# Key and query loads gated one by one on the next batch's scores, weights in six portions

## The chip, the core and the metric

One NeuronCore of a Trainium2 chip runs the whole program. The metric is the device time in microseconds (us) of one execution, lower is better. PE is the matmul engine (PEld its weight loads), DVE, ACT and POOL are the vector, scalar and GpSimd engines, SP is the sync engine, which here only waits and issues DMAs.

## The reference

Two transformer layers over x of 16 batches x 112 tokens x 256, with a context of 16 x 375 x 256. Layer 0 has a linear cross-attention and a mixture of 8 experts; layer 1 has a softmax cross-attention (the "second attention") and a feed-forward with low-rank experts. The part that matters:

```python
x = x + _L1_xattn_ref(_layernorm(x), ctx_1024, Wq, bq, Wk, bk, Wv, bv, Wo, bo)
#   Q, K, V = split into 16 heads of 16;  scores = Q K^T / 4
#   weights = softmax(scores);  attn = weights V;  return attn @ Wo.T + bo
x = x + _L1_ffn_ref(_layernorm(x), wi, bi, wo, bo, lora_A, lora_B, gate_w, gate_b)
#   gates from a top-2 of 8;  inter = h wi^T + bi + (h A_e^T) B_e^T
#   out += gate_e * (relu(inter) wo^T + bo)
```

## The kernel before

The stages run one after another: first attention, routing (in which the second attention's keys are made), the experts, the second attention (its queries first, then a loop over the 16 batches from 437 to about 655 us), and the last feed-forward.

**Operands of the second attention.** Keys and queries are split into three bf16 parts each and stacked on the partitions, so that one bf16 matmul gives an exact-enough product. The parts lie in DRAM (`kparts_d`, `qparts_d`). For each batch `load_keys` brings them into `kpk` with three DMAs (for r = 3, 2, 1: 562.5, 375 and 187.5 KB) and `load_queries` into `qpk` with three more (168, 112, 56 KB), 1.46 MB in all. Both tiles have `AHEAD` = 3 slots; batch b lies in slot b % 3.

**A step of the loop.** PE's `step(n)` makes the 12 units of `transposed_scores(n, u)` (four 128x125 by 128x112 matmuls each, line L2035), and after units 2, 4, 6, 8, 10 a pair of plain scores of the next batch (`score(n + 1, j)`, L2010), from which DVE takes row maxima (L1855). ACT takes exponentials of the units (L1756, into `probs`). Each unit adds one to the semaphore `st_ps`. Then come `weigh(n, 0)` (L2048), `shift_turn(n + 1)` (L2019), the first two score pairs of batch n + 2, `weigh(n, 1)`, and `add_up` (L2061). The first pair of scores of a batch is where PE waits for its loads:

```python
if j == 0:
    pe.wait_ge(kpk_in[s].sem, kpk_in[s].at(n // AHEAD))
    pe.wait_ge(qpk_in[s].sem, qpk_in[s].at(n // AHEAD))
```

All instructions of PE stand in this order in its queue, as they do on the other engines.

**The sync queue.** It holds the loads, the stores of query parts (`store(b)`) and the weight loads, each in order. For each n it waits until all 12 units of batch n are done, which frees the slot, and issues the six loads of batch n + 3 (L725, L1599). The stores of batches 10 to 15 stand behind the loads of n = 0 to 2. Once, at n = 9, the six weights of the last feed-forward leave (L1640): lora_a, wg1, wi (1024 KB), lora_b (512 KB), wo (1024 KB), c_earlier, 2.7 MB together. They are laid over `ctx_all`, whose values of batches 0 to 7 must have been copied by then (`vz_done`). ACT waits for the weights (`w_in`) in step 13.

Of the kernel before, what the change touches and what calls it, by code (L numbers as in the profile page):

```python
# [26 lines left out]
B, SQ, SK, D, H = 16, 112, 375, 256, 16  # L27
HD = D // H
T = B * SQ
KC = D // 128  # L30
KT, NKT = 125, 3
E0, F0 = 8, 1024
CAP = T // E0
FC = F0 // 128
E1, R1 = 8, 16
# [8 lines left out]
NR = 3  # L44
# [5 lines left out]
AHEAD = 3  # L50
VW = NKT * D
# [7 lines left out]
SCORES_AFTER, OUT_AT = {2: 2, 4: 3, 6: 4, 8: 5, 10: 6}, 6  # L59
INVERT_AT, NORM_AT = 2, 3  # L60
STATS_AHEAD = 5
WEIGHTS_AT, SPLIT_FROM, TEAM_STATS, TEAM_NORMAL = 9, B - 3, B - 3, B - 2
SPREAD = (slice(0, 4), slice(4, 8), slice(8, 16))


# [10 lines left out]
class Chain:  # L76
# [11 lines left out]
    def next(self):  # L88

        self.marked += 1  # L90
        return self.sem
# [14 lines left out]
def two_layer_kernel(nc, d, out):  # L106
# [5 lines left out]
    kparts_d = dram("kparts_d", [B, KC, NR, HD, H // KC, SK], BF16)  # L112
    qparts_d = dram("qparts_d", [B, KC, NR, HD, H // KC, SQ], BF16)

    def sb(ctx, name, shape, dt=F32, side="left"):
        return ctx.enter_context(nc.sbuf_tensor(name, shape, dt, side=side))
# [525 lines left out]
    rows = sb(ctx, "rows", [SQ, 2, 2, D])  # L642
# [25 lines left out]
    kpk = sb(keys_ctx, "kpk", [128, AHEAD, H, SK], BF16, side="right")  # L668
# [3 lines left out]
    kpk_in = [sem(ctx, f"kpk_in{s}", 48) for s in range(AHEAD)]  # L672
# [43 lines left out]
        act.wait_ge(v_ps.sem, v_ps.at(b))  # L716
        act.activation(ctx_all[0:KT, b], flat[0:KT, at:at + VW], ACT.Copy).then_inc(v_done.sem, 1)

    def load_keys(sp, b):

        s = b % AHEAD
        rows_of = lambda ap, r: ap.rearrange("m r d h k -> (r d) m (h k)")[0:r * HD]
        at = 0
        for r in (3, 2, 1):
            sp.dma_start(kpk[at:at + r * HD, s].rearrange("p (m h) k -> p m (h k)", m=KC),  # L725
                         rows_of(kparts_d[b], r)).then_inc(kpk_in[s].sem, 16)
            at += r * HD

    stage = ExitStack()
    block = stage.enter_context(nc.Block())  # L730
# [240 lines left out]
    @block.sync  # L971
    def _(sp):
        for b in range(AHEAD):
            load_keys(sp, b)
        with sp.Fori(0, E0 // 2 - 1) as i:
            for s in range(2):
                sp.wait_ge(fc2_ps.sem, fc2_ps.at(2 * i + s))
                sp.dma_start(we[:, s], d["we"][2 * i + 2 + s]).then_inc(we_in[s].sem, 16)
# [212 lines left out]
    used = [0]  # L1191

    def over_values(shape):

        size = int(np.prod(shape[1:]))
        view = ctx_all[:].rearrange("p b w -> p (b w)")[0:shape[0], used[0]:used[0] + size]
        used[0] += size
        assert used[0] <= B * VW
        names = "abcd"[:len(shape) - 1]
        spec = "p (" + " ".join(names) + ") -> p " + " ".join(names)  # L1200
        return view.rearrange(spec, **dict(zip(names, shape[1:])))

    wi = over_values([128, KC, F0])
    wo = over_values([128, FC, D])
    la = over_values([128, KC, E1 * R1])
    lb = over_values([E1 * R1, F0])
    wg1 = over_values([128, KC, E1])
    earlier = over_values([SQ, E1, E1])
    covered = (used[0] - 1) // VW
    TEAMS = [range(0, 2), range(2, 6), range(6, 10), range(10, 14), range(14, 16)]  # L1210
    NT, MOST = len(TEAMS), 4
    hn = over_values([SQ, MOST, D])
# [21 lines left out]
    low1_0 = sb(root, "low1_0", [E1 * R1, 2, 2 * SQ], F32R)  # L1234
    low21_0 = sb(root, "low21_0", [E1 * R1, 2, 2 * SQ], F32R)
    bo_f, bg1 = rows1[:, D:2 * D], rows1[:, 2 * D:]
    weights = [(la, "lora_a"), (wg1, "wg1"), (wi, "wi"), (lb, "lora_b"), (wo, "wo"), (earlier, "c_earlier")]
    tile_sum = sb(ctx, "tile_sum", [KT, KC, HC * SQ])
    half_sum = sb(ctx, "half_sum", [KT, KC, HC * SQ])
    probs = sb(ctx, "probs", [KT, KC, NKT, HC * SQ])  # L1240
# [10 lines left out]
    w_in = sem(root, "w_in", 16)  # L1251
# [23 lines left out]
    vz_done = sem(ctx, "vz_done")  # L1275
    st_ps = sem(ctx, "st_ps", UNITS)
# [313 lines left out]
    @block.sync  # L1590
    def _(sp):
        def load_queries(b):

            s = b % AHEAD
            rows_of = lambda ap, r: ap.rearrange("m r d h q -> (r d) m (h q)")[(NR - r) * HD:]
            sp.wait_ge(q_out[b % 2].sem, q_out[b % 2].at(b // 2))
            at = 0
            for r in (3, 2, 1):
                sp.dma_start(qpk[at:at + r * HD, s].rearrange("p (m h) q -> p m (h q)", m=KC),  # L1599
                             rows_of(qparts_d[b], r)).then_inc(qpk_in[s].sem, 16)  # L1600
                at += r * HD

        def store(b):
            i, s = divmod(b, 2)
            sp.wait_ge(qp1_done.sem, qp1_done.at(i))
            sp.wait_ge(qp2_done.sem, qp2_done.at(i))
            sp.wait_ge(qp3_done.sem, qp3_done.at(i))
            if i:
                sp.wait_ge(q_out[s].sem, q_out[s].at(i - 1))
            sp.dma_start(qparts_d[b].rearrange("m r d h q -> (d h) (m r) q"),  # L1610
                         qp[:, i, :, :, s * SQ:(s + 1) * SQ].rearrange("p m r q -> p (m r) q"))\
                .then_inc(q_out[s].sem, 16)

        sp.wait_ge(added.sem, added.at(E0 - 1))
        for g, part in enumerate(GROUPS):
            sp.dma_start(x_all[:, part], by_token(sum_d)[:, part]).then_inc(x2_in[g].sem, 16)
        sp.dma_start(halves[:], d["c_halves"]).then_inc(tables2_in.sem, 16)
        sp.wait_ge(ones_done.sem, ones_done.at(0))
        for s in range(1, AHEAD):
            sp.dma_start(kpk[ROWS:, s], kpk[ROWS:, 0]).then_inc(tables2_in.sem, 16)  # L1620
        for b in range(2):
            store(b)
        for b in range(2):
            load_queries(b)
        for b in range(2, 4):
            store(b)
        load_queries(2)
        for b in range(4, 10):
            store(b)
        for n in range(B):  # L1630
            if n + AHEAD < B:
                sp.wait_ge(st_ps.sem, st_ps.at(n))
                load_keys(sp, n + AHEAD)
                load_queries(n + AHEAD)
            for b in range(10 + 2 * n, min(12 + 2 * n, B)):
                store(b)
            if n == WEIGHTS_AT:
                sp.wait_ge(vz_done.sem, vz_done.at(covered))
                for dst, name in weights:
                    sp.dma_start(dst[:], d[name]).then_inc(w_in.sem, 16)  # L1640

    def unit(u):

        m, rest = divmod(u, NKT * (HC // HU))
        return (m, *divmod(rest, HC // HU))
# [48 lines left out]
    def _(act):  # L1694
# [23 lines left out]
        def zero_padded(n):  # L1718

            act.wait_ge(v_done.sem, v_done.at(n))  # L1720
            if n >= 2:
                act.wait_ge(pv_ps.sem, pv_ps.at(n - 2))
            src = ctx_all[0:KT, n].rearrange("p (t g h e) -> p t g h e", t=NKT, h=2, e=HD)
            for h in range(2):
                ins = act.activation(vz[:, n % 2, :, :, h, h * HD:(h + 1) * HD], src[:, :, :, h], ACT.Copy)
            ins.then_inc(vz_done.sem, 1)
# [13 lines left out]
        def add_bias(n):  # L1740

            act.wait_ge(au_done.sem, au_done.at(n))
            if n:
                act.wait_ge(wo1_ps.sem, wo1_ps.at(n - 1))
            for m in range(KC):
                ins = act.activation(aT1[:, m], au[:, m], ACT.Identity, bias=bv1[:, m:m + 1])
            ins.then_inc(aT1_done.sem, 1)

        def step(n):
            for u in range(UNITS):  # L1750
                m, t, g = unit(u)
                act.wait_ge(st_ps.sem, st_ps.at(n, u + 1))
                if t == 0 and g == 0 and n:
                    act.wait_ge(pv_ps.sem, pv_ps.at(n - 1, m + 1))
                    act.wait_ge(tile_sum_done.sem, tile_sum_done.at(n - 1, 2 * (m + 1)))
                act.activation(probs[:, m, t, g * HU * SQ:(g + 1) * HU * SQ],  # L1756
                               banks[B_ST[u % 3]][0:KT, 0:HU * SQ], ACT.Exp, scale=SCALE)\
                    .then_inc(exp1_done.sem, 1)
                if u == 5 and n:
                    add_bias(n - 1)  # L1760
                if u == 8 and n + 1 < B:
                    zero_padded(n + 1)
                if u == 2 and n >= SPLIT_FROM:
                    if n == SPLIT_FROM:
                        act.wait_ge(w_in.sem, w_in.at(len(weights), 0))
                        for p in range(2):
                            act.wait_ge(q_out[p].sem, q_out[p].at(PAIRS - 1))
                    for k in SPLITS_OF[n]:
                        split_high(act, k)
                if n + 1 == B:  # L1770
                    if u == 1:
                        team_turned(act, 0)
                    if u == 4:
                        low_high(act, 0)
                    if u == 6:
                        gate_exp(act, 0)
            if n + 1 < B:
                spread_shift(n + 1)
# [5 lines left out]
        for n in range(B):  # L1784
            step(n)
# [680 lines left out]
```

## Time and profile before

| | us |
|---|---|
| median of 3 runs | 805.25 |
| lowest, highest | 801.63, 809.89 |
| the profiled execution: time | 802.6 |
| its span in the trace | 800.7 |

The span is that of the instructions; the time has about 2 us more around it. Times in the rows are us from the span's start. In a timeline, neighbouring instructions of one kind are merged into one row (x2 is two of them); the brackets hold the idle time of the engine before it and what ended that. "issue" means that nothing that the profile shows was missing.

### The profile page before, as it was taken

What the parts mean: (1) busy time and instruction counts of PE and PEld (TensorE: products, weight loads), DVE (VectorE), ACT (ScalarE), POOL (GpSimd) and SP (SyncE); (2) the same over time, 40 slices, a digit from 0 to 9 for tenths busy, and PEclk for the clock granted to TensorE, in tenths of its full rate; (3) what the DMA queues carried; (4) which work ended last, traced back from release to release, by engine and by line L of the source; (5) the groups of instructions that cost most, each with busy time, mean ns of one, the idle gap of its engine ahead of it and who ended that gap; (6) DMA issues with size and microseconds to landing.
All of it is one profiled execution on the core that took longest, in us unless ns stands there. A gap on an engine that the chain in (4) does not pass through costs nothing. (4 is left out here: it accounts for less than half of the span.)

```text
span 800.7 us, 16596 instructions
## 1 busy us (share of the span) xinstructions
PE 720.1 (90%) x6421; PEld 609.7 (76%) x6421; DVE 511.8 (64%) x1262; ACT 331.8 (41%) x685; POOL 302.0 (38%) x222
## 2 busy tenths in 40 slices
PE   4899999949998999999878999899978887999997
PEld 3678888724587889988666777777766786898997
DVE  4689888768862233313457777777758758577564
ACT  2122222117833112221336787677857742423223
POOL 2233343327841323222532867677656400000000
PEclk9999999969999999999988999999999999999999
DMA  9994000124777445541642787486953000000000
GB/s 299 358 165 48 23 24 24 47 73 145 202 175 139 140 142 167 190 130 12 128 105 49 125 155 143 91 144 113 255 99 59 2 3 8 4 25 0 25 12 24
DMA packets 64474, 81.54 MB, mean 102 GB/s; under 512 B 31890, under 2 KB 54802, under 8 KB 62834
## 3 DMA queue, kind: packets, MB, share of 16 engines
q1 hardware_dynamic: 61170, 72.22, 38.0%
q0 software_dynamic: 2816, 3.67, 2.5%
q10 hardware_dynamic: 416, 4.65, 1.5%
q8 instruction: 50, 0.82, 0.5%
q14 instruction: 22, 0.18, 0.1%
HBM read 60.45 MB, written 19.31 MB: 100 GB/s over the span
## 5 line engine op out<-in xcount | busy, mean ns | idle before, releaser
L1855 DVE TENSOR_REDUCE mx<-psum 112x2 f32<-112x750 f32 x128 | 113.3, 925 | 17.7 <-PE psum L2010 17.0
L1756 ACT ACTIVATE probs<-psum 125x448 f32<-125x448 f32 x192 | 92.8, 542 | 19.2 <-PE psum L2035 17.4
L556 PE MATMUL psum<-w_parts,c_parts 128*125 128x512 f32 x288 | 75.0, 414 | 10.8 <-DVE w_parts L424 10.4
L1675 POOL TENSOR_TENSOR half_sum<-probs 125x896 f32<-125x896 f32 x30 | 62.5, 2083 | 57.4 <-ACT probs L1756 57.4
L2035 PEld LDWEIGHTS psum<-qpk,kpk 128*125 128x125 bf16 x768 | 62.9, 141 | 22.6 <-issue 14.7
L2035 PE MATMUL psum<-qpk,kpk 128*125 128x112 bf16 x768 | 69.4, 227 | 9.0 <-issue 7.0
L556 PEld LDWEIGHTS psum<-w_parts,c_parts 128*125 128x125 f32 x288 | 54.6, 193 | 25.1 <-DVE w_parts L424 10.4
L2010 PE MATMUL psum<-kpk,qpk 96*112 96x375 bf16 x256 | 64.2, 344 | 9.4 <-DVE mx L1855 8.8
L1681 POOL TENSOR_TENSOR tile_sum<-half_sum,probs 125x896 f32<-125x896 f32 x30 | 62.6, 2087 | 2.4
L1148 PE MATMUL psum<-we,hT 128*112 128x256 f32 x256 | 60.9, 400 | 0.0
L995 ACT ACTIVATE hT<-psum,b 128x224 f32<-128x224 f32 x64 | 25.1, 443 | 77.8 <-PE psum L1133 77.8
L1148 PEld LDWEIGHTS psum<-we,hT 128*112 128x112 f32 x256 | 47.8, 189 | 10.9
L1412 ACT ACTIVATE ctx_all<-psum,cols 128x448 f32<-128x448 f32 (+1 forms) x40 | 22.4, 560 | 80.4 <-PE psum L1576 80.3
L1028 POOL DMA_INDIRECT sum_d<-outs,idx_add x16 | 29.8, 1864 | 63.4 <-DVE outs L1084 51.0
L803 PE MATMUL psum<-ctx_all,wk 128*128 128x375 f32 x128 | 45.5, 500 | 6.4 <-PEq L248 4.9
L2324 PE MATMUL psum<-wo_parts,hs_parts 128*112 128x256 f32 x384 | 48.1, 281 | 3.1 <-DVE wo_parts L1367 3.0
L1133 PE MATMUL psum<-rT,we 128*128 128x224 f32 x256 | 49.8, 353 | 0.9 <-ACT rT L986 0.9
L1080 DVE TENSOR_TENSOR tmp<-psum,b 112x512 f32<-112x512 f32 x8 | 5.5, 691 | 69.1 <-PE psum L1148 69.1
L1133 PEld LDWEIGHTS psum<-rT,we 128*128 128x128 f32 x256 | 48.4, 190 | 1.5 <-issue 1.1
L2324 PEld LDWEIGHTS psum<-wo_parts,hs_parts 128*112 128x112 f32 x384 | 46.1, 175 | 3.9 <-DVE wo_parts L1367 3.2
L1524 DVE SCALAR_TENSOR_TENSOR ctx_all<-psum,neg_bi,ctx_all 128x448 f32<-128x448 f32 (+1 forms) x40 | 23.5, 589 | 37.7 <-PE psum L1585 37.3
L708 PE MATMUL psum<-wv,ctx_all 128*125 128x256 f32 x192 | 47.1, 406 | 0.0
(231 smaller groups left out, 1468.9 us busy)
## 6 DMA issues: line engine op xcount, KB each, us to landing
we<-in_we SPq DMA_DIRECT2D x6, 2048.0 KB, 8.6
kparts_d<-kp SPq DMA_DIRECT2D x16, 562.5 KB, 4.8
kpk<-kparts_d SPq DMA_DIRECT2D x16, 562.5 KB, 6.0
ctx_all<-in_ctxT SPq DMA_DIRECT2D x16, 375.0 KB, 5.2
kpk<-kparts_d SPq DMA_DIRECT2D x16, 375.0 KB, 7.7
we<-in_we ACTq DMA_DIRECT2D x2, 2048.0 KB, 11.9
kpk<-kparts_d SPq DMA_DIRECT2D x16, 187.5 KB, 8.5
qparts_d<-qp SPq DMA_DIRECT2D x16, 168.0 KB, 3.0
```

Of the source, the lines that this page charges most:

```text
L556: ins = pe.matmul(banks[B_KV[t]][0:KT, :], parts_of[:, x, k, t * KT:(t + 1) * KT], w_parts[:, k, w], start=(k == 0 and (x, w) == SPLIT[0]) ...
L708: ins = pe.matmul(flat[0:KT, at + t * D:at + (t + 1) * D], ctx_of(b)[:, k, t * KT:(t + 1) * KT], wv1[:, k], start=(k == 0), stop=(k == KC ...
L803: ins = pe.matmul(banks[B_K[2 * s + m]][:, 0:SK], wk1[:, k, m * 128:(m + 1) * 128], ctx_of(n)[:, k], start=(k == 0), stop=(k == KC - 1))
L1133: ins = pe.matmul(banks[B_F[g]][:, (f % 2) * CAP:(f % 2 + 1) * CAP], we1[:, s, k, f * 128:(f + 1) * 128], rT[:, s, k], start=(k == 0), sto ...
L1148: ins = pe.matmul(banks[B_OUT[s]][0:SQ, h * D:(h + 1) * D], hT[:, s, f, h * SQ:(h + 1) * SQ], we2[:, s, f], start=(f == 0), stop=(f == FC ...
L1675: pool.tensor_tensor(half_sum[:, m], probs[:, m, 0], probs[:, m, 1], ALU.add)\
L1681: pool.tensor_tensor(tile_sum[:, m], half_sum[:, m], probs[:, m, 2], ALU.add)\
L1756: act.activation(probs[:, m, t, g * HU * SQ:(g + 1) * HU * SQ], banks[B_ST[u % 3]][0:KT, 0:HU * SQ], ACT.Exp, scale=SCALE)\
L1855: dve.tensor_reduce(mx[:, n % 2, H + 2 * j:H + 2 * j + 2], psum[0:SQ, first:first + 2, 0:SK], AX.X, ALU.max)\
L2010: ins = pe.matmul(banks[B_S[j % 2] + h][0:SQ, 0:SK], qpk[0:ROWS, s, 2 * j + h], kpk[0:ROWS, s, 2 * j + h], start=True, stop=True)
L2035: ins = pe.matmul(banks[B_ST[u % 3]][0:KT, c * SQ:(c + 1) * SQ], kpk[:, s, h, t * KT:(t + 1) * KT], qpk[:, s, h], start=True, stop=True)
L2324: ins = pe.matmul(y_of(i, s), hs_parts[:, x, f, s * SQ:(s + 1) * SQ], wo_parts[:, w, f], start=(f == 0 and (x, w) == SPLIT[0]), stop=(f == ...
```

## The change

`load_keys` is cut into its three DMAs. In the loop over n each of them waits for a unit of the *next* batch: the first for one finished unit of batch n + 1, the second for three, the third for four; the three query loads follow after five. Before, all six waited for the last unit of batch n. The weights no longer leave together at n = 9 but behind the loads of n = 3 to 8: wi in two halves (512 KB each), wo in two halves, lora_a with wg1 (136 KB), lora_b with c_earlier (540 KB). Each portion waits for the values that it covers. ACT's wait in step 13 counts eight DMAs instead of six.

```diff
+KEYS_AT, QUERIES_AT = (1, 3, 4), 5
-    def load_keys(sp, b):
-
-        s = b % AHEAD
-        rows_of = lambda ap, r: ap.rearrange("m r d h k -> (r d) m (h k)")[0:r * HD]
-        at = 0
-        for r in (3, 2, 1):
-            sp.dma_start(kpk[at:at + r * HD, s].rearrange("p (m h) k -> p m (h k)", m=KC),
-                         rows_of(kparts_d[b], r)).then_inc(kpk_in[s].sem, 16)
-            at += r * HD
+    def load_keys(sp, b, r):
+
+        s, at = b % AHEAD, sum(range(r + 1, NR + 1)) * HD
+        sp.dma_start(kpk[at:at + r * HD, s].rearrange("p (m h) k -> p m (h k)", m=KC),
+                     kparts_d[b].rearrange("m r d h k -> (r d) m (h k)")[0:r * HD]).then_inc(kpk_in[s].sem, 16)
...
+        def load_weight(name, half=None):
+
+            dst, covered = next((t, c) for t, w, c in weights if w == name)
+            sp.wait_ge(vz_done.sem, vz_done.at(covered))
+            rows = slice(None) if half is None else slice(half * dst.shape[1] // 2, (half + 1) * dst.shape[1] // 2)
+            sp.dma_start(dst[:, rows], d[name][:, rows]).then_inc(w_in.sem, 16)
...
         for n in range(B):
             if n + AHEAD < B:
-                sp.wait_ge(st_ps.sem, st_ps.at(n))
-                load_keys(sp, n + AHEAD)
+                for r, u in zip((3, 2, 1), KEYS_AT):
+                    sp.wait_ge(st_ps.sem, st_ps.at(n + 1, u))
+                    load_keys(sp, n + AHEAD, r)
+                sp.wait_ge(st_ps.sem, st_ps.at(n + 1, QUERIES_AT))
                 load_queries(n + AHEAD)
             for b in range(10 + 2 * n, min(12 + 2 * n, B)):
                 store(b)
-            if n == WEIGHTS_AT:
-                sp.wait_ge(vz_done.sem, vz_done.at(covered))
-                for dst, name in weights:
-                    sp.dma_start(dst[:], d[name]).then_inc(w_in.sem, 16)
+            if n in (3, 4):
+                load_weight("wi", n - 3)
+            if n in (5, 6):
+                load_weight("wo", n - 5)
+            if n == 7:
+                load_weight("lora_a")
+                load_weight("wg1")
+            if n == 8:
+                load_weight("lora_b")
+                load_weight("c_earlier")
...
-                        act.wait_ge(w_in.sem, w_in.at(len(weights), 0))
+                        act.wait_ge(w_in.sem, w_in.at(len(weights) + 2, 0))
```

## Rows read from the trace of the kernel before

**Rows 1.** Windows: busy us and (instructions) by engine, then clock, DMA share, GB/s.

```profile
437.00:655.00 218.00, 196.19 (x3405) 162.45 (x3404) 163.83 (x246) 152.48 (x334) 138.52 (x78) 0.98 0.57 109
```

**Rows 2.** Waits of PE from 437 to 655: us in total, times, longest.

```profile
PE psum L2035 <- issue: 7.0, 3, 3.5
```

**Rows 3.** Timeline of the sync engine: start, us, operation, count.

```profile
492.33 1.25 SPq L725 DMA_DIRECT2D kpk<-kparts_d  x3
...
519.34 2.27 SPq L725 DMA_DIRECT2D kpk<-kparts_d  x3
...
531.50 1.25 SPq L725 DMA_DIRECT2D kpk<-kparts_d  x3
532.79 1.53 SPq L1599 DMA_DIRECT2D qpk<-qparts_d  x3
544.17 1.57 SPq L725 DMA_DIRECT2D kpk<-kparts_d  x3
...
568.48 1.89 SPq L725 DMA_DIRECT2D kpk<-kparts_d  x3
...
580.64 1.25 SPq L725 DMA_DIRECT2D kpk<-kparts_d  x3
...
597.83 1.25 SPq L725 DMA_DIRECT2D kpk<-kparts_d  x3
```

**Rows 4.** Timeline of PE behind its three long stalls.

```profile
503.27 0.27 PE L2035 MATMUL psum<-qpk,kpk 128*125 128x112 bf16 x2 [1.83 <-issue]
...
589.59 0.33 PE L2035 MATMUL psum<-qpk,kpk 128*125 128x112 bf16 x3 [3.50 <-issue]
...
608.59 0.50 PE L2035 MATMUL psum<-qpk,kpk 128*125 128x112 bf16 x6 [1.67 <-issue]
```

**Rows 5.** DMA queues (packets, MB, share): the instruction queue, whole span, then 586.4 to 586.6.

```profile
q8 instruction: 50, 0.82, 0.5%
...
q8 instruction: 1, 0.02, 41.1%
```

**Rows 6.** Windows, columns as in rows 1: the quick and the slow part.

```profile
531.47:536.07 4.60, 4.56 (x122) 3.39 (x121) 3.95 (x6) 2.53 (x6) 4.52 (x3) 1.00 0.78 147
536.34:545.78 9.44, 8.34 (x131) 6.76 (x129) 7.11 (x9) 7.13 (x16) 6.44 (x4) 1.00 0.55 95
```

**Rows 7.** Timeline of PE over one step.

```profile
533.62 0.85 PE L2010 MATMUL psum<-kpk,qpk 96*112 96x375 bf16 x4
...
536.07 0.67 PE L2035 MATMUL psum<-qpk,kpk 128*125 128x112 bf16 x8
...
537.79 0.62 PE L2035 MATMUL psum<-qpk,kpk 128*125 128x112 bf16 x8
...
543.75 0.39 PE L2035 MATMUL psum<-qpk,kpk 128*125 128x112 bf16 x4
```

**Rows 8.** Windows, columns as in rows 1: DMA share within a burst.

```profile
534.00:540.00 6.00, 5.58 (x117) 4.57 (x116) 4.76 (x6) 4.81 (x9) 3.40 (x3) 1.00 1.03 172
```

**Rows 9.** DMA issues, us to landing: median of 13; issued at 571.4, 582.9, 533.7, 558.6.

```profile
qpk<-qparts_d SPq DMA_DIRECT2D x13, 56.0 KB, 8.5
...
qpk<-qparts_d SPq DMA_DIRECT2D x1, 56.0 KB, 11.5
...
qpk<-qparts_d SPq DMA_DIRECT2D x1, 56.0 KB, 7.8
...
qpk<-qparts_d SPq DMA_DIRECT2D x1, 56.0 KB, 9.1
...
qpk<-qparts_d SPq DMA_DIRECT2D x1, 56.0 KB, 8.9
```

**Rows 10.** Windows, columns as in rows 1: behind the three stalls.

```profile
504.60:508.00 3.40, 3.40 (x30) 2.67 (x32) 1.77 (x3) 1.75 (x4) 2.47 (x2) 0.50 0.15 28
608.60:612.00 3.40, 3.40 (x48) 3.01 (x51) 1.73 (x2) 3.10 (x7) 2.45 (x2) 1.00 0.02 5
590.00:593.40 3.40, 3.40 (x34) 2.71 (x28) 2.54 (x3) 1.98 (x4) 0.32 (x1) 0.50 0.02 7
```

More of the change, by code:

```diff
@@ L61 @@
 STATS_AHEAD = 5
-WEIGHTS_AT, SPLIT_FROM, TEAM_STATS, TEAM_NORMAL = 9, B - 3, B - 3, B - 2
+KEYS_AT, QUERIES_AT = (1, 3, 4), 5
+SPLIT_FROM, TEAM_STATS, TEAM_NORMAL = B - 3, B - 3, B - 2
 SPREAD = (slice(0, 4), slice(4, 8), slice(8, 16))
@@ L973, in _ @@
         for b in range(AHEAD):
-            load_keys(sp, b)
+            for r in (3, 2, 1):
+                load_keys(sp, b, r)
         with sp.Fori(0, E0 // 2 - 1) as i:
@@ L1201, in over_values, with weight_over_values @@
         return view.rearrange(spec, **dict(zip(names, shape[1:])))
[L1203 to L1209, printed above, removed]
+    weights = []
+    def weight_over_values(shape, name):
+        tile = over_values(shape)
+        weights.append((tile, name, (used[0] - 1) // VW))
+        return tile
+    wi = weight_over_values([128, KC, F0], "wi")
+    wo = weight_over_values([128, FC, D], "wo")
+    la = weight_over_values([128, KC, E1 * R1], "lora_a")
+    lb = weight_over_values([E1 * R1, F0], "lora_b")
+    wg1 = weight_over_values([128, KC, E1], "wg1")
+    earlier = weight_over_values([SQ, E1, E1], "c_earlier")
     TEAMS = [range(0, 2), range(2, 6), range(6, 10), range(10, 14), range(14, 16)]
@@ L1236, in two_layer_kernel @@
     bo_f, bg1 = rows1[:, D:2 * D], rows1[:, 2 * D:]
-    weights = [(la, "lora_a"), (wg1, "wg1"), (wi, "wi"), (lb, "lora_b"), (wo, "wo"), (earlier, "c_earlier")]
     tile_sum = sb(ctx, "tile_sum", [KT, KC, HC * SQ])
```

## The prediction

> **What bounds the kernel now.** I read, in this order: the chain that ended last, the windows by stage, the list of waits in the stage that the change touches, and then the timelines of the sync queue and of PE there. The chain covers only the stage behind the second attention, so it says nothing of the stage in question. The window over that stage does: in the batch loop, 437 to 655 us, PE is busy 196.2 of 218 us, the next engine (DVE) 163.8 [rows 1]. It is bound by PE, and what PE waits for is what counts. Beside many short waits the list has 7.0 us of "issue" in only three pieces of up to 3.5 us [rows 2], when nothing that the profile shows was missing.
>
> The sync queue's timeline gives the loop's pitch, because each batch's key loads leave when the last transposed score of a batch is done. From 519.34 to 531.50 is 12.16 us, and 568.48 to 580.64 is the same [rows 3]. Four steps are longer: the two from 492.33 to 519.34 take 27.01, 531.50 to 544.17 is 12.67, 580.64 to 597.83 is 17.19. Excesses: 2.69 + 0.51 + 5.03 = 8.2 us. One more stall of 1.67 us ends at 608.59, in the next step [rows 4]. Together 9.9 us of the run are irregular.
>
> **What these stalls are.** In the three long ones PE stops in the middle of a batch's transposed scores, operands ready [rows 4]. Just before, the load burst is running. The 50 packets of the instruction queue carry 0.82 MB, and PE has 6421 weight loads and 6421 matmuls: one 16 KB packet for about 257 of them. The last such packet ahead of the 3.50 us stall starts only at 586.4 to 586.6, and PE goes on 3 us later, at 589.59 [rows 5]. So I read the three stalls as PE running out of instructions, because a fetch waited behind the 1.46 MB of key and query loads. Where the burst falls matters: from the last transposed score to the next batch's first (531.47 to 536.07) PE takes 243 weight loads and matmuls in 4.6 us; from there to the next such point (536.34 to 545.78) it takes 260 in 9.44 us [rows 6]. Today the burst leaves at 531.50, at the start of the quick part, so a page of 257 can be used up in less than 5 us.
>
> **Part 1, the loads move: what it removes.** The first load now waits for unit 0 of the next batch. The burst then lies over the slow part. A fetch asked for after it began is not needed for 257 instructions, and the slow part has 260: the next page is not missed before the point at 545.78 where PE needs the loads themselves. I take all 9.9 us away (a price between 0, if the stalls have another cause, and 9.9).
>
> **What it adds.** Batch n+3's first two scores stand at the end of step n+1. PE reaches them 2.12 us after the old issue point (533.62 against 531.50) [rows 3, 7], so one pitch later the loads have 12.16 + 2.12 = 14.28 us to land. Sync issues 0.42 us after the last unit's first matmul starts (543.75, issue at 544.17) [rows 3, 7]; unit 0 starts at 536.07, so the new first issue is about 536.5, 5.0 us later than 531.50. That leaves 14.28 - 5.04 = 9.24 us.
>
> Do the loads need less if they leave "one by one"? The gates are units 0, 2, 3 and 4. Unit 3 starts at 537.79 and with unit 4 takes 0.62 us [rows 7], so all gates are open 1.9 us after the first. Six issues at some 0.47 us take 2.3 us already (531.50 to the last one at 533.7) [rows 3]; now they take about 3.1. The DMA engines are full through this, 1.03 of their nominal capacity from 534 to 540 [rows 8]. Capacity limits the burst, not the issuing. Thus the last 56 KB land as late after the first issue as they do now: their median time to landing is 8.5 us, so 2.2 + 8.5 = 10.7 us [rows 3, 9]. The shortest and longest of the plain bursts are those of 580.64 and 531.50: 2.3 + 7.8 = 10.1 and 2.2 + 9.1 = 11.3 [rows 3, 9]. The median holds two bursts near the weights; without them I take 10.6. One burst bears out the need point: issued 568.48 among the weights, its last load, issued at 571.4, took 11.5 us and landed at 582.8 [rows 3, 9], 568.48 + 14.28 is 582.76, and the pitch over it stayed 12.16.
>
> So PE now waits for the loads at each of 13 batches: 10.6 - 9.24 = 1.4 us, and with 0.1 for waking 1.46 us; 13 x 1.46 = 19.0 us. Bounds: 10.1 gives 0.96 and 12.5 us, 11.3 gives 2.16 and 28 us. I take the mean. No cover is left for this wait: PE's queue behind it holds the four score matmuls, weigh(n, 1), add_up and unit 0 of the next batch, and everyone waits for those. DVE's next two maxima, its reciprocal (behind PE's sums) and ACT's first exponential all follow PE, so nothing later in the step absorbs it. What was late before (the fetches) hides under the same wait.
>
> **Part 2, the weights move.** 2.7 MB left in one go behind batch 12's loads, and the pitch from 568.48 to 580.64 was undisturbed, so taking them away there gains nothing. Six portions now leave behind the loads of batches 6 to 11, 136 to 540 KB each. At the burst's own pace (1.46 MB in some 9.5 us) 512 KB are 3.5 us of DMA time. They are queued behind that batch's queries and done by 5.0 + 0.9 + 9.5 + 3.5 = 18.9 us, just as the next burst begins (13.6 + 5.0 us), so they don't delay it. Weights in the ring do stretch the query load ahead of them: the last query load of the burst that they follow now took 8.9 us [rows 9], so that burst 11.1, 0.5 over the others. I add 0.4 us for each of five of the six batches (bounds 0 and 0.6; the smallest portion is left out): 2.0 us. ACT's wait for the weights stands in batch 13 either way, long after they have landed: nothing. The stores of query parts are queued on sync behind the gated loads in steps 0 to 2, 5 us later; the first reader is batch 10's load, six steps later: nothing.
>
> **Part 3, the clock.** After the stalls of 1.83 and 3.50 us the granted clock was 0.50 (1.2 GHz) from 504.6 to 508.0 and from 590.0 to 593.4, after that of 1.67 us it stayed at 1.00 (2.4 GHz) [rows 4, 10]. 5.03 - 3.50 = 1.5 us and 2.69 - 1.83 = 0.9 us are its price. Waits of 1.5 us lie below both. I take nothing for it, and the removed 9.9 us hold the two old ones.
>
> **The sum**, against the profiled execution's own 802.6 us: 802.6 - 9.9 + 19.0 + 2.0 = 813.7; **814 us**. The three timed runs have a median of 805.25 (801.6 to 809.9). I expect them to differ by how many fetches came late, which the new order would end, so I don't shift the sum.
>
> **A rule weighed.** The rows above show PE standing with a fetch packet still to come. The Trainium skill ("Runtime: NRT & Kernel Launch", Instruction fetch mechanics) says that the instruction memory is refilled in blocks of 16 KiB, 256 instructions, which the trace bears out (257), but that crossing a block is mostly hidden. ("DMA: Bandwidth & Descriptors", Queues, rings and completion order) adds that each DMA engine alternates between its queues packet by packet. By both a fetch would not wait out a burst and nothing would be there to remove; that is rival B.
>
> **The rivals.**
> A. *The loads land in time after all.* With the queue less deep when each leaves, or the DMA engines quicker beside the slow part, the burst would need under 9.3 us instead of 10.6; nothing is then added: 802.6 - 9.9 + 1 = 794 us. Against it: plain bursts of 10.1 to 11.3, and a DMA share near 1 over the quick part and into the slow one [rows 8]. Chance 0.17.
> B. *The stalls have another cause or only move* (a fetch behind the weight portions, say), and the waits for the loads come on top: 802.6 + 19 + 2 = 824 us. Against it: all three long stalls lie behind a burst in progress, none in an undisturbed stretch. Chance 0.12.
> C. *The waits cost clock too.* If the burst needs 11 us rather than 10.6, PE waits 1.9 us at a time, as long as it did before the clock fell at 504.6, and each wait is followed by such a stretch at 0.50, at 0.9 us a time: 814 + 13 x 0.9 = 826 us, before the longer waits themselves. This ends clearly slower; the 11 us are the point from which it decides. Chance 0.13.
> The change not doing what it says is part of the forecast: the gates open within 1.9 us and the "one by one" is still one burst.
>
> **How the numbers follow.** Forecast 0.58, A 0.17, B 0.12, C 0.13. The forecast's own range is 804 to 821 (12.5 to 26 us added). Leaving out a tenth on each side, the whole runs from 798 to 826. This kernel's measurement can't tell less than about 1% from no change; 1% is 797.2 to 813.3. The forecast lies at the edge: half of it (0.29) slower, half the same; B and C slower; A mostly faster: faster 0.14, same 0.32, slower 0.54.
>
> **What would show it.** Right: in each of 13 steps PE idles 1 to 2 us before the score line L2010's first pair, released by a DMA and no longer by DVE; the pitch is a regular 13.6 us; the first load leaves 5 us later in the step and the last one still lands 10 to 11 us after it; the "issue" stalls in the transposed scores are gone. Wrong: a pitch of 12.2 us (A), stalls of over 1.5 us that stay in the transposed scores (B), a clock of 0.50 in several stretches between 440 and 650 (C).

## The result, and the profile after

The changed kernel takes 823.2 us (median of 4 runs, 819.1 to 828.8) against 804.2 us (801.6 to 809.9; with a fourth run beside the three that gave 805.25): ratio 1.023, 95% interval [1.017, 1.028]. It is slower, by about 2%. The profiled execution has a span of 821.6 us, 20.9 us over that of before (the span, not the time, is what the accounts below go by).

The list of PE's waits in the loop (us in total, times, longest):

```profile
PE psum L2029 <- DMA qpk<-qparts_d: 21.6, 13, 2.7
PE psum L2029 <- DVE mx L1874: 8.6, 25, 0.4
PE psum L2054 <- ACT probs L1775: 1.6, 2, 0.8
```

L2029 is the score line (L2010 before), L2054 the transposed scores (L2035). The 7.0 us of "issue" in three pieces [rows 2] are no longer in this list; 13 waits for the query loads have taken their place, 1.66 us each. The sync queue's timeline shows the new pitch and where the weight portions stand:

```profile
462.96 1.97 SPq L723 DMA_DIRECT2D kpk<-kparts_d  x3
...
477.48 1.97 SPq L723 DMA_DIRECT2D kpk<-kparts_d  x3
479.55 1.30 SPq L1603 DMA_DIRECT2D qpk<-qparts_d  x3
...
490.99 1.97 SPq L723 DMA_DIRECT2D kpk<-kparts_d  x3
493.07 1.30 SPq L1603 DMA_DIRECT2D qpk<-qparts_d  x3
494.42 0.42 SPq L1612 DMA_DIRECT2D ctx_all<-in_wi  x1
506.63 2.19 SPq L723 DMA_DIRECT2D kpk<-kparts_d  x3
...
520.71 1.97 SPq L723 DMA_DIRECT2D kpk<-kparts_d  x3
```

Where sync issued every 12.16 us in the undisturbed steps [rows 3], it is now 14.52, 13.51, 15.64 and 14.08. The timeline of PE shows what these are made of:

```profile
474.58 0.82 PE L2029 MATMUL psum<-kpk,qpk 96*112 96x375 bf16 x4 [2.32 <-DMA qpk<-qparts_d]
475.34 1.36 PE L2067 MATMUL psum<-probs,vz 125*32 125x112 f32 x48
...
477.01 0.67 PE L2054 MATMUL psum<-qpk,kpk 128*125 128x112 bf16 x8
...
502.41 0.82 PE L2029 MATMUL psum<-kpk,qpk 96*112 96x375 bf16 x4 [2.11 <-DMA qpk<-qparts_d]
503.17 2.08 PE L2067 MATMUL psum<-probs,vz 125*32 125x112 f32 x48
...
505.92 1.10 PE L2054 MATMUL psum<-qpk,kpk 128*125 128x112 bf16 x8
```

From 463 to 477.5 the step is 12.16 + 2.32 to within 0.04 us: nothing else is in it. From 491 to 506.6 it is 12.16 + 2.11 + 1.4: after that wait the same 48 matmuls of `weigh` take 2.08 us instead of 1.36. There the granted clock is 0.50 instead of 1.00. Three such stretches of 3.4 us lie in the loop, and two more behind it (a longer one at the loop's start stands in both kernels). In these windows the clock stands third from the end:

```profile
503.60:507.00 3.40, 3.40 (x68) 2.97 (x62) 1.13 (x2) 0.37 (x1) 0.00 (x0) 0.51 0.00 0
548.00:551.40 3.40, 3.40 (x64) 2.75 (x53) 0.74 (x1) 0.98 (x2) 0.00 (x0) 0.50 0.12 21
575.30:578.70 3.40, 3.40 (x60) 2.78 (x62) 1.78 (x2) 0.47 (x1) 0.41 (x1) 0.50 0.00 1
...
677.70:681.10 3.40, 3.40 (x12) 2.42 (x11) 0.00 (x0) 0.60 (x2) 0.00 (x0) 0.50 0.00 0
694.80:698.20 3.40, 3.14 (x9) 2.83 (x10) 3.29 (x14) 0.00 (x0) 1.01 (x1) 0.50 0.00 0
```

The landing times of the query loads, 13 each (KB, median us from issue to landing), are shorter than before (8.5 for the last, [rows 9]), but that load leaves 3.0 us after the first one instead of 2.2:

```profile
qpk<-qparts_d SPq DMA_DIRECT2D x13, 112.0 KB, 7.5
qpk<-qparts_d SPq DMA_DIRECT2D x13, 56.0 KB, 7.6
```

3.0 + 7.6 = 10.6 us, where 10.7 (10.6 without the weights' neighbours) had been read off the kernel before. Taken burst by burst, it is 10.3 to 11.7 us from the first issue to the last landing, 10.8 in the mean. In each of the 13 steps PE's first score matmul starts 0.24 or 0.25 us after that landing.

### The profile page after: what moved, and what is told of

The parts are those of the page before. It is cut to its first block and busy times, and to the rows that moved or that the text cites. A ratio compares the mean times of both kernels' runs of the same rounds, so it can differ in the third digit from the quotient of the medians.

```text
span 821.6 us, 16611 instructions
## 1 busy us (share of the span) xinstructions
PE 728.1 (89%) x6421; PEld 614.7 (75%) x6421; DVE 512.0 (62%) x1262; ACT 331.3 (40%) x685; POOL 302.0 (37%) x222
## 5 line engine op out<-in xcount | busy, mean ns | idle before, releaser
L2029 PE MATMUL psum<-kpk,qpk 96*112 96x375 bf16 x256 | 63.4, 340 | 32.2 <-DMA qpk<-qparts_d 21.6
L2054 PEld LDWEIGHTS psum<-qpk,kpk 128*125 128x125 bf16 x768 | 63.1, 143 | 15.8 <-issue 7.8
L2054 PE MATMUL psum<-qpk,kpk 128*125 128x112 bf16 x768 | 70.0, 229 | 1.7 <-ACT probs L1775 1.6
L2029 PEld LDWEIGHTS psum<-kpk,qpk 96*112 96x112 bf16 x256 | 26.1, 133 | 41.7 <-issue 24.8
```

The source lines that it names most:

```text
L2029: ins = pe.matmul(banks[B_S[j % 2] + h][0:SQ, 0:SK], qpk[0:ROWS, s, 2 * j + h], kpk[0:ROWS, s, 2 * j + h], start=True, stop=True)
L2054: ins = pe.matmul(banks[B_ST[u % 3]][0:KT, c * SQ:(c + 1) * SQ], kpk[:, s, h, t * KT:(t + 1) * KT], qpk[:, s, h], start=True, stop=True)
```

## The experiments

The edits are against the changed kernel. Times are medians of the timed runs; each ratio is to the kernel before on the same chip.

**Loads alone** (weights together again at n = 9):

```diff
-            if n in (3, 4):
-                load_weight("wi", n - 3)
...
+            if n == 9:
+                for name in ("lora_a", "wg1", "wi", "lora_b", "wo", "c_earlier"):
+                    load_weight(name)
```

> The gated key and query loads alone; the six weights leave together behind the loads of n = 9, as before. Theory 1 (the late landing is the cost, the weight portions add 0.4 us to five bursts): 13 waits of 1.4 to 1.7 us for the query loads, 2 us less than the changed kernel, 820 to 822 us, ratio to before 1.020. Theory 2 (the portions behind the loads cause a good part, by stretching bursts and calling up the lower clock): 812 us or less, ratio 1.01, and no stretch of 0.50 in the loop.

827.9 us, ratio 1.034 [1.022, 1.047]: not faster than the whole change. PE's wait list has

```profile
PE psum L2022 <- DMA qpk<-qparts_d: 23.8, 13, 2.9
```

and the granted clock has four stretches of 0.50 within the loop. The gated loads alone make the whole loss, so theory 2 is out. This run is no clean test of the 0.4 us per portion, because the 2.7 MB at n = 9 now stand between late bursts: two of the four waits behind them are 2.9 and 2.45 us. A comparison within the changed kernel is closer. Its six waits for bursts with a weight portion behind them average 1.78 us, the other seven 1.57; with all gates at unit 1 it is 1.59 against 1.48, with the later gates 2.69 against 2.65. A portion costs some 0.05 to 0.2 us, and with waits that spread from 0.8 to 2.7 us even that is not sure.

**Weights alone** (loads at the last unit of batch n as before):

```diff
-                for r, u in zip((3, 2, 1), KEYS_AT):
-                    sp.wait_ge(st_ps.sem, st_ps.at(n + 1, u))
-                    load_keys(sp, n + AHEAD, r)
-                sp.wait_ge(st_ps.sem, st_ps.at(n + 1, QUERIES_AT))
+                sp.wait_ge(st_ps.sem, st_ps.at(n))
+                for r in (3, 2, 1):
+                    load_keys(sp, n + AHEAD, r)
```

> The loads wait for the last unit of batch n as before; only the weights leave in six portions. Theory 1: no wait for a DMA (3.7 us of slack), so within 3 us of before, ratio 0.997 to 1.005, with stalls from late instruction fetches still there. Theory 2 (the portions are a good part of the cost): ratio 1.01 or more.

807.7 us, ratio 1.010 [1.005, 1.015]: above the range of theory 1, at the lower end of theory 2's. No wait for a DMA, but 8.3 us of "issue":

```profile
PE psum L2053 <- issue: 6.4, 3, 2.8
PE psum L2079 <- issue: 1.4, 1, 1.4
PE psum L2028 <- issue: 0.5, 1, 0.5
```

The kernel before had 7.0 us in the transposed scores and 0.7 elsewhere in its one trace, so 0.6 us more is too little to say that the portions make late fetches worse; where the 1% comes from stays open. Under the gated loads these stalls are gone.

**All six gates at unit 1** (`KEYS_AT, QUERIES_AT = (1, 1, 1), 1`):

> All six loads wait for the first unit of the next batch (gates 1, 1, 1 and 1 instead of 1, 3, 4 and 5). Theory 1 (DMA capacity sets the length of the burst, not the spacing of the issues): as the changed kernel within 3 us, waits of 1.4 to 1.7 us in all 13 steps. Rival (the spacing counts): the last load leaves 0.9 us earlier and lands earlier by as much, 13 x 0.9 = 11 us faster than the changed kernel, 812 us.

823.8 us, ratio 1.031 [1.019, 1.044], the time of the changed kernel. The waits hardly differ:

```profile
PE psum L2029 <- DMA qpk<-qparts_d: 19.9, 13, 2.1
```

19.9 us is 0.13 us less per step, not the 0.9 us by which the last load was expected to leave and land earlier. What counts is when the burst begins. "One by one" is one burst.

**Gates later** (`KEYS_AT, QUERIES_AT = (3, 5, 6), 7`):

> Gates 3, 5, 6 and 7 instead of 1, 3, 4 and 5: the first load leaves 1.1 us later. Theory 1: each of the 13 waits grows by 1.1 us to some 2.7 us, 14 us slower than the changed kernel from that, and if waits of over 1.8 us call up the lower clock, at 1.6 us each time, in most steps, up to 20 us more: 837 to 857 us. If the clock doesn't answer to the length of the wait, 837 us with some three stretches at 0.50 as in the changed kernel.

845.2 us, ratio 1.058 [1.043, 1.073].

```profile
PE psum L2029 <- DMA qpk<-qparts_d: 34.7, 13, 2.9
```

Each wait is 2.67 us, 1.0 more than in the changed kernel, for a gate 1.1 us later. That is 13 us. The loop takes 23 us longer than in the changed kernel (244.2 against 221.1, by the traces), and the other 10 us fit the clock: nine stretches of 0.50 in the loop instead of three, the first twice as long, from 459.8 to 466.6. Columns as above:

```profile
459.80:466.60 6.80, 5.99 (x88) 4.85 (x92) 1.79 (x2) 1.19 (x3) 0.39 (x1) 0.50 0.23 33
493.90:497.30 3.40, 3.40 (x69) 3.07 (x63) 1.42 (x2) 0.00 (x0) 0.00 (x0) 0.50 0.03 6
```

**Halved key loads, late and early.** Key loads of batches 3 to 15 bring the first half of each row only; the rest of the slot keeps an older batch's values, so these two leave work out. The late one has the change's gates, the early one those of the kernel before.

```diff
+        part = slice(0, H // KC * SK // (2 if b >= AHEAD else 1))
-        sp.dma_start(kpk[at:at + r * HD, s].rearrange("p (m h) k -> p m (h k)", m=KC),
-                     kparts_d[b].rearrange("m r d h k -> (r d) m (h k)")[0:r * HD]).then_inc(kpk_in[s].sem, 16)
+        sp.dma_start(kpk[at:at + r * HD, s].rearrange("p (m h) k -> p m (h k)", m=KC)[:, :, part],
+                     kparts_d[b].rearrange("m r d h k -> (r d) m (h k)")[0:r * HD, :, part]).then_inc(kpk_in[s].sem, 16)
```

> The changed kernel, but the key loads of batches 3 to 15 bring only the first half of each row (work left out), so a burst moves 0.9 MB instead of 1.46 MB, at the same gates and by as many issues. Theory 1: the burst ends within 7.5 us, no wait for it is left, no stall from a late fetch either, pitch 12.16 us in every step, 792 to 796 us, ratio 0.985 to 0.99. Rival (the late issue itself costs something beside the wait, or the stalls had nothing to do with the loads): 800 us or more.

> The same halved key loads (work left out) at the old place, behind the last unit of batch n, weights in six portions. If late fetches are due to the length of the burst, they wait only some 5 us at most and the stalls go: 793 to 797 us. If it is the place of the burst in the quick part that matters, whatever its length, stalls of 1 to 4 us stay in some steps: 798 to 805 us.

Late: 795.7 us, ratio 0.990 [0.985, 0.994]. Early: 794.4 us, ratio 0.989 [0.984, 0.995]. Neither has a wait for a DMA nor an "issue" stall in the loop. The last load's landing, late one first:

```profile
qpk<-qparts_d SPq DMA_DIRECT2D x13, 56.0 KB, 3.8
```

```profile
qpk<-qparts_d SPq DMA_DIRECT2D x13, 56.0 KB, 4.5
```

The late burst now lasts 3.0 + 3.8 = 6.8 us, under the 9.24 that PE leaves it. The sync queue of the late one has its undisturbed pitch, 533.29 to 545.44:

```profile
533.29 1.97 SPq L724 DMA_DIRECT2D kpk<-kparts_d  x3
545.44 1.97 SPq L724 DMA_DIRECT2D kpk<-kparts_d  x3
```

Two things follow. A late place costs nothing by itself: the loop takes 194.3 us in both, so all of its cost is the wait and what the wait brings with it. And the stalls of the kernel before need the *length* of the burst: at the old place a burst of 0.9 MB causes none.

**After the shift turn** (all six loads, full, wait for `turn_ps` of batch n + 1, some 2 us after the last unit):

```diff
-                for r, u in zip((3, 2, 1), KEYS_AT):
-                    sp.wait_ge(st_ps.sem, st_ps.at(n + 1, u))
-                    load_keys(sp, n + AHEAD, r)
-                sp.wait_ge(st_ps.sem, st_ps.at(n + 1, QUERIES_AT))
+                sp.wait_ge(turn_ps.sem, turn_ps.at(n + 1))
+                for r in (3, 2, 1):
+                    load_keys(sp, n + AHEAD, r)
```

> All six loads wait for the shift turn of the next batch, some 2 us after the last unit, weights in six portions. The burst should end 12.7 us after the last unit against 14.28 needed. Theory 1: no wait for a DMA, fetch stalls in fewer steps because half of the quick part is over: 793 to 802 us, ratio 0.985 to 1.0. Rival (the place in the quick part doesn't matter for fetches): as before, 803 us.

796.5 us, ratio 0.990 [0.983, 0.996], with no wait for a DMA and two short stalls:

```profile
PE psum L2066 <- issue: 1.3, 2, 0.9
```

This kernel differs from "weights alone" (1.010, 8.3 us of stalls) only in the place of the burst, so for a burst of full length the place does matter. That fetches behind it are needed later, once part of the quick part is over, is the reading that fits; it is not shown.

**Halves by heads.** The keys of heads 0 to 7 are not read after unit 5 of batch n, so their loads can leave six units earlier; those of heads 8 to 15 and the queries follow after the last unit. The full work, in nine loads.

```diff
+    def load_keys(sp, b, m):
+        s, at = b % AHEAD, 0
+        for r in (3, 2, 1):
+            sp.dma_start(kpk[at:at + r * HD, s].rearrange("p (m h) k -> p m (h k)", m=KC)[:, m],
+                         kparts_d[b].rearrange("m r d h k -> (r d) m (h k)")[0:r * HD, m])\
+                .then_inc(kpk_in[s].sem, 16)
+            at += r * HD
...
+                sp.wait_ge(st_ps.sem, st_ps.at(n, UNITS // KC))
+                load_keys(sp, n + AHEAD, 0)
+                sp.wait_ge(st_ps.sem, st_ps.at(n))
+                load_keys(sp, n + AHEAD, 1)
                 load_queries(n + AHEAD)
```

> A version that could win: the keys of heads 0 to 7 are loaded when the first six units of batch n are done (nobody reads that half of the slot any more), those of heads 8 to 15 and the queries after the last unit. Full work. Theory 1: two shorter bursts, the second of some 6 us in the quick part; no wait for a DMA; fetch stalls fewer but possible: 793 to 800 us, ratio 0.985 to 0.997. Rival: twelve issues of smaller packets' groups cost more DMA time and the first part slows something in the slow part: 803 us or more.

791.5 us (790.5 to 794.2), ratio 0.985 [0.979, 0.990]: faster than both kernels, by 1 to 2% against the one before. In the wait list of PE the first lines are

```profile
PE psum L2032 <- DVE mx L1877: 9.2, 26, 0.6
PE psum L2057 <- ACT probs L1778: 1.6, 2, 0.8
```

and neither DMA nor "issue" stands there. The pitch is 12.15 and 12.16 from the second burst on (the x6 of a row are the key loads of both halves, 4.7 us apart):

```profile
509.21 6.98 SPq L724 DMA_DIRECT2D kpk<-kparts_d  x6
...
521.36 5.90 SPq L724 DMA_DIRECT2D kpk<-kparts_d  x6
...
533.52 6.65 SPq L724 DMA_DIRECT2D kpk<-kparts_d  x6
```

The two largest key loads of a half land in 3.8 and 4.1 us (in the stage's list of issues):

```profile
kpk<-kparts_d SPq DMA_DIRECT2D x24, 281.2 KB, 3.8
kpk<-kparts_d SPq DMA_DIRECT2D x24, 187.5 KB, 4.1
```

From its own first issue, the first half is complete after 4.8 to 5.9 us, and the second with the queries after 6.4 to 7.8.

**The second half late, and the weights at n = 9**, both on top of the halves by heads: one waits with the second half and the queries for `st_ps.at(n + 1, 1)`, the other has the `n == 9` edit shown first.

> As e7, but the keys of heads 8 to 15 and the queries wait for the first unit of the next batch, 5 us later. That second part (0.9 MB) ended within 7.5 us when it stood alone in e5, and 9.24 us are left. Theory 1: no wait for a DMA, no fetch stall, pitch 12.16 throughout, 790 to 796 us, equal to e7 within the measurement. Rival (a late place costs something of its own): 800 us or more.

> As e7, with the six weights together behind the loads of n = 9, as before the change. Theory 1: in e7 the loads have slack enough, so the order of the weights makes no difference in the undisturbed steps, but 2.7 MB in one go delay one or two fetches by up to 6 us and may stall PE once: 791 to 797 us. Rival (the portions are what cleared the stalls in e7): stalls in several steps, 800 us or more.

795.6 us, ratio 0.987 [0.983, 0.990], and 794.1 us, ratio 0.985 [0.982, 0.988]. Neither has a wait for a DMA or an "issue" stall. The weights' order is indifferent there, and so is the place of the second half. Of these three the plain halves have the lowest median, but their ratios' intervals overlap.

## Why the prediction was right, and where it was off

It forecast 814 us, slower, by waits for the query loads that take the place of stalls from late fetches. The direction and this mechanism were right, the size was not: 823.2 us lies above the forecast's own 804 to 821, in the part of the whole range (to 826) that belonged to rivals B and C. Also, 804 to 821 is not what the stated bounds give: 12.5 and 28 us of waits lead to 805 without and 823 with the 2.0 us for the weights.

The loop can be measured on its own, from the first transposed-score matmul to the last step's `weigh`. Four kernels have no stall, no wait for a load and no stretch at 0.50 behind the loop's start: the halved loads, late and early, the halves by heads, and the same with the weights at n = 9. All four take 194.3 us there. Against this floor:

| kernel | loop, us | over 194.3 | waits for loads | stretches at 0.50 | rest |
|---|---|---|---|---|---|
| before | 203.2 | 8.9 | none | 2 | |
| changed | 221.1 | 26.8 | 21.6 | 3 | 5.2 |
| loads alone | 224.6 | 30.3 | 23.8 | 4 | 6.5 |
| all gates at unit 1 | 216.6 | 22.3 | 19.9 | 1 | 2.4 |
| gates later | 244.2 | 49.9 | 34.7 | 9, one double | 15.2 |

The steps of the prediction in turn:

- *9.9 us of stalls go.* They went: no "issue" in the loop's list. They were worth 8.9 us, stretches at 0.50 included. The last one, of 1.67 us, cost only 0.7 in the end: from the last burst's first issue to the last `weigh` the kernel before takes 42.5 us, the early halved loads 41.8.
- *13 waits of 1.46 us, 19.0 us.* 13 waits, 21.6 us. The time that PE leaves the loads was 9.3 us in ten of the 13 steps and 9.5 to 9.9 in the others, against 9.24 forecast. Waking took 0.24 us, not 0.1, and the mean burst 10.8 us, not 10.6. The spacing of the issues did nothing (gates all at unit 1: 19.9 us of waits).
- *Weights, 2.0 us.* Oversized: some 0.05 to 0.2 us a portion, contained in the waits above. Together with the waits the sum was 21.0 against 21.6. That is luck: the waits were taken too small, this term too large.
- *Clock, nothing.* The mis-sized term, and the largest. Three of the 13 waits (2.11, 2.68 and 1.85 us) were followed by a stretch at 0.50. The first of them cost 1.4 us in its own step and, from 506.63 to 520.71, 14.08 - 12.16 - 1.66 = 0.3 in the next: some 1.6 us each, 5 us together. The step failed because it took all waits at the mean of 1.5 us, below the 1.83 after which the clock had fallen; the waits spread from 0.8 to 2.7. This was rival C's mechanism, and the sign named for C, a clock of 0.50 in several stretches, did appear, in three steps and not in all 13. The table shows how it grows: nine stretches at waits of 2.3 to 2.9. What ties them to the waits is the order in time and this count.
- *Not in the sum:* behind the loop, two more stretches at 0.50. The stage from the loop's end to the end of the span takes 160.3 us before and 163.7 after, with the same instructions:

```profile
640.40:800.70 160.30, 148.41 (x1197) 139.02 (x1196) 102.72 (x265) 50.98 (x103) 3.73 (x4) 1.00 0.04 13
```

```profile
657.90:821.60 163.70, 151.70 (x1197) 141.44 (x1196) 102.81 (x265) 51.02 (x103) 3.73 (x4) 0.98 0.04 12
```

It isn't the waits' doing: the halves by heads, without any of them, have 163.6 there, the gates all at unit 1 and the later gates 161.1 and 161.2. But the one trace of the kernel before has no stretch there, and each of the eleven others has one or two, so whether the change has a part in it stays open. In the profiled pair 3.3 us come from this. Of the difference of the medians, 19.0 us, it may be less; that split stays open too.

The account of the spans: 21.6 (waits) + 4.9 (clock in the loop) - 8.9 (stalls) = 17.6, of the 17.9 us by which the loop grew. With 3.3 behind the loop and 0.3 less ahead of it these make the 20.9.

**The rivals.** "In time after all" had the price right (794; 795.7 and 794.4 with halved loads) and the condition too, a burst under 9.24 us. It is just not met by 1.46 MB. "The stalls have another cause or only move" fell: they vanish under the gated loads, and at the old place when the burst is shorter; what PE lacked in them is told below. "The waits cost clock too" came true for three steps, as told above.

**The rule weighed.** Of what the Trainium skill ("Runtime: NRT & Kernel Launch", Instruction fetch mechanics) says, the blocks of 256 instructions agree with the trace (257), and "mostly hidden" holds for most of the 50 packets, but the few that were not hidden cost 8.9 us of 801. That a DMA engine alternates packet by packet (the Trainium skill, "DMA: Bandwidth & Descriptors", Queues, rings and completion order) didn't keep the fetches from being late. What holds them within the engine isn't shown by any run here; that stalls need a long burst is.

That the missing thing is an instruction block rested on one packet of the instruction queue [rows 5]. The kept traces say more. From the loop's start on, the kernels before, weights alone and after the shift turn have eleven "issue" stalls of PE over 0.3 us, and each ends 2.65 to 3.1 us after a 16 KB packet of that queue starts. For the longest one in weights alone, here is PE's row, and below it the instruction queue in the window from 603.0 to 603.2:

```profile
606.01 0.79 PE L2053 MATMUL psum<-qpk,kpk 128*125 128x112 bf16 x6 [2.77 <-issue]
```

```profile
q8 instruction: 1, 0.02, 41.5%
```

And the stalls stand at block borders. The PE instructions recorded ahead of each of the eleven (weight loads, matmuls and those of its sequencer) number 5769, 6025, 6537 (twice), 7305, 7817, 8329, 8585, 9353 and 9865 (twice): every difference is a whole multiple of 256. That settles what was missing.

The same counts give an estimate of how late the fetches leave. Behind the loop, with the DMA engines nearly idle, a packet starts when PE has about 1.1 blocks left to run. Measured from that point, 14 of the loop's 25 fetches leave over 5 us late in the kernel before, the latest 7.6 us. None does in the halved loads, early or late, or in the halves by heads. In the changed kernel it is 5 of 25, the latest again 7.6 us, without a stall: there PE needs such a block later or waits for the loads meanwhile, as the prediction had it.

## What to carry to other kernels

A transfer's deadline is read from the first instruction that needs it: from the queue's issue point to that instruction one pitch later is the time that the loads have. Subtract the length of the whole burst, from the first issue to the last landing, and the rest is the slack. With the DMA engines full, as here, spreading the issues over 2 us didn't shorten that, and a gate that is later than the slack (here 3.7 us) makes a wait in every step. If PE stalls with nothing missing while a long burst runs, try a shorter burst first: free a buffer in halves and load each half when its last reader is done.

## What the runs showed that I had not expected

- The clock's answer to waits isn't all or nothing. Waits of 2.32 us (474.6) and 1.79 us passed without a stretch at 0.50, 1.85 us (575.0) didn't. With waits of 2.3 to 2.9 us nine stretches came in 13 steps. The changed kernel pays about a quarter of its waits again in clock; the three kernels with waits of 1.5 to 1.8 us on average had one, three and four stretches. Nor does every stretch follow such a wait: with the second half late, one lies from 613.0 to 616.4 us, and no wait of PE over 0.8 us stands anywhere in the loop ahead of it.
- A burst of 0.9 MB at the same place as one of 1.46 MB caused no late fetch in 13 steps, where the full one cost up to 5.0 us in a single step. The harm isn't proportional to the bytes.
- The largest miss was the term set to nothing. The mean wait lay below the one after which the clock had fallen, but single waits lay above it, and 4.9 us came from three of them.
